# Attention: how far the products of the maximum run ahead of the scores, two items against one item and six key tiles

## The reference, cut to what matters

```
hn = _layernorm(x, ln1_g, ln1_b)
q = (hn @ wq + bq).reshape(b, s, NH, D).transpose(0, 2, 1, 3)
k = (hn @ wk + bk).reshape(b, s, NH, D).transpose(0, 2, 1, 3)
v = (hn @ wv + bv).reshape(b, s, NH, D).transpose(0, 2, 1, 3)
scores = jnp.einsum('bhqd,bhkd->bhqk', q, k) / jnp.sqrt(jnp.float32(D))
attn = jax.nn.softmax(scores, axis=-1)
o = jnp.einsum('bhqk,bhkd->bhqd', attn, v)
```

## Time and profile before

| | us |
|---|---|
| median of three runs | 3656.47 |
| the profiled execution | 3660.14 |
| its span, first to last instruction | 3658.3 |
| PE busy (share of span) | 3051.2 (83%) |
| DVE busy | 2599.6 (71%) |
| ACT busy | 1732.7 (47%) |

### The profile page before, as it was taken

The page is one execution under the profiler, slowest core; times in us unless marked ns, Lnnn a source line. Parts: engine busy times, 40 slices in busy tenths (PEclk is TensorE's granted clock), DMA queues, the critical chain, the costliest instruction groups (busy, mean ns, idle before and its releaser), DMA issues. The chain is left out here.

```text
span 3658.3 us, 43277 instructions
## 1 busy us (share of the span) xinstructions
PE 3051.2 (83%) x12860; PEld 1452.0 (40%) x12860; DVE 2599.6 (71%) x3622; ACT 1732.7 (47%) x2113; POOL 816.1 (22%) x397
## 2 busy tenths in 40 slices
PE   5768788798797775999999999999999957769994
PEld 3333234243343332433333333333333324658883
DVE  5527989889889896998989898989899539101111
ACT  2225554554554541276767676767677820101110
POOL 2204555455455465000000000000000015220003
PEclk9879899899898887599999999999999965579997
DMA  4532121111121114644444444444444044044554
GB/s 150 162 114 87 64 74 71 64 64 67 60 75 67 54 71 64 119 63 63 62 63 62 63 62 63 62 63 62 63 62 62 10 115 124 18 148 163 171 170 129
DMA packets 230405, 306.67 MB, mean 84 GB/s; under 512 B 111467, under 2 KB 179332, under 8 KB 215748
## 3 DMA queue, kind: packets, MB, share of 16 engines
q1 hardware_dynamic: 225988, 291.60, 35.0%
q0 software_dynamic: 4224, 12.59, 1.2%
HBM read 240.38 MB, written 63.21 MB: 83 GB/s over the span
## 5 line engine op out<-in xcount | busy, mean ns | idle before, releaser
L694 DVE TENSOR_REDUCE attn_mx<-attn_pX 128x1 f32<-128x512 f32 x2048 | 1269.9, 682 | 153.8 <-PE attn_pX L608 153.7
L674 ACT ACTIVATE attn_pr<-attn_pS 128x1024 f32<-128x1024 f32 x1024 | 991.8, 1021 | 514.8 <-PE attn_pS L621 513.5
L608 PE MATMUL attn_pX<-attn_ks,attn_qs 48*128 48x512 f32 x2048 | 767.3, 500 | 79.2 <-DMA attn_vs<-v_d 25.1
L1142 PE MATMUL mamba_pY<-mamba_g,mamba_ident 128*128 128x512 f32 x1024 | 527.9, 665 | 212.0 <-DVE mamba_g L1266 211.9
L1253 DVE TENSOR_TENSOR_SCAN mamba_h<-mamba_pA,mamba_hs,mamba_db 128x512 f32<-128x512 f32 x512 | 617.6, 1263 | 98.4 <-ACT mamba_pA L996 92.8
L608 PEld LDWEIGHTS attn_pX<-attn_ks,attn_qs 48*128 48x128 f32 x2048 | 312.3, 193 | 792.4 <-DVE attn_mx L694 717.4
L937 POOL TENSOR_TENSOR mamba_db<-mamba_bq,mamba_u 128x2048 f32<-128x2048 f32 x128 | 577.8, 4514 | 72.0 <-DVE mamba_u L1213 71.7
L996 ACT ACTIVATE mamba_pA<-mamba_dt,mamba_an 128x512 f32<-128x512 f32 x512 | 351.7, 691 | 452.7 <-DVE mamba_h L1253 452.5
L631 PE MATMUL attn_pO<-attn_pr,attn_vs 128*17 128x512 f32 x4096 | 554.2, 614 | 0.8 <-ACT attn_pr L674 0.7
L621 PE MATMUL attn_pS<-attn_qs,attn_ks 50*128 50x512 f32 x2048 | 467.6, 414 | 23.7 <-issue 19.0
L1142 PEld LDWEIGHTS mamba_pY<-mamba_g,mamba_ident 128*128 128x128 f32 x1024 | 211.7, 213 | 513.7 <-DVE mamba_g L1266 269.7
(11 more groups left out here) (170 smaller groups left out, 2036.3 us busy)
## 6 DMA issues: line engine op xcount, KB each, us to landing
mamba_bq<-bc_d SPq DMA_DIRECT2D x64, 1024.0 KB, 4.7
attn_ks<-parts_d SPq DMA_DIRECT2D x192, 256.0 KB, 9.1
exp_w<-in_w SPq DMA_DIRECT2D x46, 1024.0 KB, 4.9
attn_vs<-v_d SPq DMA_DIRECT2D x32, 544.0 KB, 15.8
parts_d<-proj_qp SPq DMA_DIRECT2D x32, 512.0 KB, 3.0
attn_qs<-parts_d SPq DMA_DIRECT2D x192, 64.0 KB, 8.3
attn_qs<-attn_mt SPq DMA_DIRECT2D x512, 1.0 KB
oraw_d<-attn_oe SPq DMA_DIRECT2D x32, 256.0 KB, 2.1
```

The source lines that it names most:

```text
L608: pe.matmul(pX[bank(s, n)][:, :], QS[slot][rows, pair, qt * P:(qt + 1) * P], KS[slot][rows, pair, part * BANK:(part + 1) * BANK], start=Tr ...
L674: act.activation(PR[2 * (kt % 2) + pair][:, :, :], pS[pair][:, :, :], ACT.Exp, scale=HD ** -0.5).then_inc(p_sb, 1)
L694: dve.tensor_reduce(MX[:, col:col + 1], pX[bank(s, n)][:, :], AX.X, ALU.max).then_inc(x_max, 1)
L1142: mm = pe.matmul(pY[j][:, :], ident[:, :], G[k % 2][:, n, :], start=False, stop=(q == NQ - 1 and n == QN - 1))
```

## The change

`LEAD = 6 * SM_KT` = 24 products. PE makes all 64 products of item 0 and only the first 24 of item 1 before the loop. At each key tile of item s it still issues four products, at the same four places, but they are those 24 further on in item s + 1: key tiles 0 to 9 make products 24 to 63 of item s + 1, key tiles 10 to 15 make products 0 to 23 of item s + 2. In the last item but one, key tiles 0 to 9 still have products, and in the last there are none. On DVE, `split` and `turned` of item s + 1 move behind the last 40 reductions of item s + 1. SP's code is unchanged.

```
+    LEAD = 6 * SM_KT
...
                 scores_max(0, 0, 0, NSM)
-                scores_max(0, 1, 0, NSM)
+                scores_max(0, 1, 0, LEAD)
...
+                def maxima_ahead(i, s, left, n0, n1):
+
+                    if n0 + LEAD < NSM:
+                        if left >= 1:
+                            scores_max(i, s + 1, n0 + LEAD, n1 + LEAD)
+                    elif left >= 2:
+                        scores_max(i, s + 2, n0 + LEAD - NSM, n1 + LEAD - NSM)
...
-                            if left >= 2:
-                                scores_max(i, s + 2, n + pair * SM_KT // 4, n + (pair + 1) * SM_KT // 4)
+                            maxima_ahead(i, s, left, n + pair * SM_KT // 4, n + (pair + 1) * SM_KT // 4)
                         values(i, s, kt)
-                        if left >= 2:
-                            scores_max(i, s + 2, n + SM_KT // 2, n + SM_KT)
+                        maxima_ahead(i, s, left, n + SM_KT // 2, n + SM_KT)
...
-                maxima(0, 1, 0, NSM)
+                maxima(0, 1, 0, LEAD)
 
                 def body(i, s, left):
                     if left >= 1:
+                        maxima(i, s + 1, LEAD, NSM)
                         split(i, s + 1)
                         turned(i, s + 1)
                     if left >= 2:
-                        maxima(i, s + 2, 0, NSM)
+                        maxima(i, s + 2, 0, LEAD)
```

## The result

The changed kernel takes **3637.0 us** (median of 5 runs, 3635.6 to 3638.8), the kernel before 3659.5 beside it. The ratio is 0.9937, 95% interval 0.9924 to 0.9950: 0.6% faster, outside the predicted range. The profiled execution has a span of 3634.0 us.

What follows compares the result with a forecast made beforehand. PE was taken as the bound, with DVE 0.21 us behind per key tile. Terms -23.9 + 6.9 + 4.2 + 12.1 + 9.0 = +8.3 us gave 3665 us, 0.23% above the median of 3656.5; range 3648 to 3686.

Steps and rivals of the forecast that it cites:

- The jumps keep their price: At the loop's six jumps back: their cost stays as before, no change counted, apart from 0.60 us each for the split.
- part 3: DVE's split moves from key tile 0 to 10: six jumps and item 0 each pay 0.60 us, +4.2 us.
- rival E: Maximum rows on time and shorter half clock at the jumps, three stretches saving 7 us: 3643 us; chance 0.05, faster.
- PE has no idle time, nothing hides a late row: Attention's key tiles: PE is the bound at 2.69 us, so late maximum rows cost in full, +12.1 us.
- opening: Attention's key tiles: DVE reduces for 2.48 us, then idles 0.21 us for PE, so PE is the bound.
- part 4: Head of key tile 15: maximum rows come at 14.87 against 14.39, 0.48 us late in 23 items, +12.1 us in all.
- Part 1: Before the loop: 40 reductions of 0.599 us leave DVE's stretch, -23.9 us, first scores at 1497.2.
- Parts 2 and 5: Last item but one: products in 10 key tiles, +6.9 us; rows 5.0 us late plus half clock, +9.0 us.
- Rival B: Maximum rows over a microsecond late in every item, through slow issues on SP: sum +35, 3692 us; chance 0.22, slower.
- Rival D: PE's clock falls at each of 30 waits for maximum rows: +105 us at least, about 3770; chance 0.03.

## Why the prediction was wrong

**The jumps keep their price** (part 3, and the reason that rival E was given 0.05) is the step that failed: it was put at nothing, and the six jumps became 21.2 us cheaper. Rival E, 3643, came nearest to the 3637, with "nothing speaks for it but chance". I read one jump and took its price for a property of jumps. Six were in the trace, each with a second stall, and half clock alternating between two lengths was a sign of something unexplained. The runs with idle instructions show that the price follows the place of the code, and the instruction packets show why: PE reaches the end of the block it has jumped into after 38 instructions before, and stands until the next one is there; after the change it gets about 118 instructions far, and the next block has come. The kernel before, shifted by 147, has 35.5 without any of the change. So this gain does not belong to what the change is for.

**PE has no idle time, nothing hides a late row** (opening and part 4) failed next, +12.1 us predicted. The lateness was sized well, 0.39 against 0.48, but free. I dismissed 652.9 us of weight loads waiting for DVE as early loads; before the fourth product of a key tile they are real, 0.47 us of PE's time (0.71 us behind the third product as a rule, 0.24 when the rows are late). With part 3's 4.2 I charged 16.3 us; the items outside the jumps' first key tiles and the last two gained 11.0. That is not the 12.1 come back: 7.8 of it lies in the six jump items. Part 3's 0.6 each for the split is 3.6 of this. Of the other 4.2, 6 x (1.14 - 0.67) = 2.8 are a second thing that part 3 missed: key tile 11, where DVE now does its split, loses 1.14 us in jump items, 0.67 in an ordinary one. DVE's first reduction starts 0.47 us behind the transposition there, 0.14 elsewhere. It is not DVE's own jump, whose branch ran 34 us earlier (2037.34, 0.06 us long), and item 0 has the 0.46 too, before anything has jumped; written out, no item has it. So it goes with the loop's first item, and the cause is open. After, DVE and PE in such a key tile:

```profile
2071.40 0.21 DVE L718 STREAM_TRANSPOSE attn_mt<-attn_ms 128x32 f32<-128x32 f32 x1
...
2071.87 3.68 DVE L701 TENSOR_REDUCE attn_mx<-attn_pX 128x1 f32<-128x512 f32 x6 [0.26 <-issue]
2072.62 0.49 PE L609 MATMUL attn_pX<-attn_ks,attn_qs 48*128 48x512 f32 x1 [0.65 <-DVE attn_mx L701]
```

**Part 1 held**: -23.9 predicted; first scores 26.8 us earlier, of which 2.9 is attention's start. **Parts 2 and 5** were 15.9 us together and came to 12.5 (+11.3 and +1.2): the wait was 4.8 us at ACT against 5.0 of lateness, but half clock lasted 6.8 us, not 13.5. The landing of 1.7 us in **part 4** was right too: with lead 5, where the scores wait for the rows in every item, they start 1.70 to 1.77 us after the last issue has started in 31 of 32 items, so the 0.3 us more that the prediction held possible didn't come. **Rival B** stayed away: the 16 issues took 10.2 to 10.5 us from first to last in 28 of 32 items. **Rival D** stayed away at this lead, though the 1.14 us that the prediction leaned on is no safe bound, as the other runs show.

Put together: the sum of +8.3 with the jumps' -21.2 is -12.9, and without the 12.1 for late rows -25.0; found were -24.5. The other errors, each of some 3 us (start, last items, DVE's delay, slow issues), cancel, which is luck.

## What to carry over

A hardware loop's jump has a price that depends on where its code lies, so any edit that adds or removes instructions ahead of or in a loop can move the time by more than what it is for (here 27 to 67 us for six jumps). Compare variants with the loop written out, or shifted by idle instructions, before crediting an edit. Written out, this kernel is 1.2% faster, and with a lead of seven or eight key tiles 1.6%. Single runs with column halves and lead 8 went lower, to 3591, but others went up to 3651.

Before a wait is charged, look for the next wait on the same engine: if a product behind it waits 0.5 us for a bank anyway, as here, the first 0.4 us of lateness cost nothing, and one key tile less of lead costs 125.

## What had not been expected of the hardware

- Two matmul groups side by side took as long as four (0.97 and 0.98 us to the next product).
- A semaphore increment on PE took 0.15 us; 256 of them took 39.6 us, of which some 22 were hidden behind a wait for loads.
- A second stall of 2.5 to 5.4 us can follow a jump's first of about 3, nine instructions later, when the code lies so that the next 16 KB of instructions are needed there.
- PE's clock fell to half behind idle times of 0.64 to 0.66 us in some variants, and not behind one of 1.20 us in another.
- Half clock lasted 75 us in a kernel whose PE issued without a gap, and 3 to 21 us behind single waits where PE had half a microsecond of slack per key tile.
